# Two PSUM reads of a routing step move from VectorE to ScalarE, and TensorE turns the numbers earlier in its step

## The chip, the cores and the metric

The kernel runs on one core of one Trainium2 chip. The metric is device microseconds of one execution, median of three runs. A core has TensorE (PE in the profile; PEld is its weight load), VectorE (DVE), ScalarE (ACT), GpSimd (POOL) and SyncE (SP, which here only issues DMAs). Each engine works through its own instructions in the order in which they were issued to it; a semaphore wait holds one engine and everything that stands behind the wait on that engine.

## The reference

The input is 16 sequences of 512 tokens with 128 features. Each sequence passes causal attention with 16 heads of 8 features, a layer norm, a product-key mixture of experts (8 heads, 32 + 32 keys, the best 8 of 64 pairs, 1,024 experts), and a second layer norm.

```python
q, k = _rope(_rms_norm(q, q_norm_w), _rms_norm(k, k_norm_w), cos, sin)
attn = softmax(where(causal, -inf, einsum('bhqd,bhkd->bhqk', q, k) * scale))
x = _layernorm(x + einsum('bhqk,bhkd->bhqd', attn, v)... @ w_proj.T)
...
xn = _rmsnorm(x, norm_w)
q = (xn @ w_q.T).reshape(b, t, H, 2, DK)
s1, i1 = top_k(einsum('bthd,hkd->bthk', q[..., 0, :], keys[:, :, 0, :]), K)
s2, i2 = top_k(einsum('bthd,hkd->bthk', q[..., 1, :], keys[:, :, 1, :]), K)
all_idx = (i1[..., :, None] * NKEYS + i2[..., None, :]).reshape(b, t, H, K * K)
all_sc = (s1[..., :, None] + s2[..., None, :]).reshape(b, t, H, K * K)
fs, pk = top_k(all_sc, K)
fi = take_along_axis(all_idx, pk, axis=-1)
hidden = gelu(einsum('btd,bthkd->bthk', xn, expert_down[fi])) * relu(fs)
x = _layernorm(x + einsum('bthk,bthkd->btd', hidden, expert_up[fi]))
```

## The kernel before, in words

One pass of the loop (`iteration`) works on up to five sequences at once, each at another stage: `b` is in attention, `nxt` is having its q and k made, `late` (b-1) is in the norm and the choice of experts, `older` (b-2) in the experts' weights, `oldest` (b-3) in the last product and norm. With 16 sequences there are 19 passes; 2 to 14 hold nearly all stages, pass 15 has no `nxt`, and pass 16 has no attention of its own. The order on each engine is written out by hand, in one function `iteration` for each engine. TensorE and ScalarE count 40 steps in a pass, one per unit of attention scores.

TensorE, at each step: the scores of the step into one of two PSUM banks `S`; at steps 27, 31, 35 and 39 (`QK_STEPS`) the transposes of `nxt`'s stacked q and k into the same two banks (`transpose_stack`); at most steps one of 32 parts of `weights(older)`, which multiplies one-hot rows of experts by their weights into a bank `G`; and `late`'s work on its selection. `turn_numbers(late, t)` transposes the chosen experts' numbers of tile t, 20 matmuls, at steps 22, 28, 34 and 35 (`NUMBER_STEPS`). `transpose_selection`, two transposes at step 35, adds the chosen scores to the same bank, `F_SEL`. Part 28 of `weights`, at step 35, waits for `rows_done`: VectorE's last four one-hot blocks of `older`.

ScalarE: at each step the exponential of the scores (`prob<-S`); at QK_STEPS the copies of q and k from the banks (`qT`, `kT_even`, `kT_odd`). The scores of step 36 go to the bank that q was turned into and wait for the copy `qT`; those of step 37 go to k's bank and wait for `kT_odd`.

VectorE: sorts out the keys and pairs of `late` (`top_keys`, `top_pairs`), and makes the one-hots and weights of `older`. After `top_pairs(late, 3)` GpSimd's `gather` finishes the last tile of numbers, while VectorE makes one-hots 28 to 31 and applies a chunk of weights. Then `decode(late)` reads `F_SEL` and splits each expert number into a low and a high part (`elo`, `ehi`) and each weight into three bf16 parts (`wpart`), and the first one-hots of that sequence follow. `eint`, the whole numbers, lies in the memory of `hot_hi`; so the trace calls it `hot_hi`.

Of the kernel before, what the change touches and what calls it, by code (L numbers as in the profile page):

```python
# [39 lines left out]
def attention_then_peer_layer(nc, x, w_qkv, w_proj, q_norm_w, k_norm_w, w_q, keys, expert_down, expert_up,  # L40
# [3 lines left out]
    ALU, ACT, AX = mybir.AluOpType, mybir.ActivationFunctionType, mybir.AxisListType  # L44

    P = 128
# [21 lines left out]
    with ctx:  # L68
# [137 lines left out]
        def signal(name, per_batch, seed=0):  # L206
            return Signal(sem(name), per_batch, seed)
# [37 lines left out]
        sel_ready = signal("sel_ready", 1)  # L245
# [10 lines left out]
        numbers_turned = signal("numbers_turned", NT)  # L256
        hid_done = signal("hid_done", NHI, 2)
        dec = signal("dec", 4, 4)
        hi_done = signal("hi_done", 4)
        hot_done = signal("hot_done", 4)  # L260
        rows_done = signal("rows_done", 1)
# [289 lines left out]
        def _(act):  # L551
# [11 lines left out]
            def hidden(b, c):  # L563
                act.wait_ge(hid_ready.sem, hid_ready.value(b, c + 1))
                act.activation(hid[:, c, :], bank_hid(c)[:, :], ACT.Gelu).then_inc(hid_done.sem, 1)  # L565

            def taken_x(b):
                act.wait_ge(xT_ready.sem, xT_ready.value(b, 1))
                act.activation(xT[:, :], bank_s("xT", 0)[:, :], ACT.Copy).then_inc(xT_done.sem, 1)
# [90 lines left out]
            def iteration(b, late, older, oldest, nxt):  # L660


                if late is not None:
                    attended(late, NG - 1)
                if b is not None:
                    taken_v(b)
                if nxt is not None:
                    taken_x(nxt)
                for n in range(NG * UNITS):
                    if b is not None:  # L670
                        exps(b, n // UNITS, [n % UNITS])
                    if n == 3:
                        if nxt is not None:
                            taken_qk(nxt, 0)
                            taken_qk(nxt, 1)
                        if late is not None:
                            taken_outputs(late)
                    if n == 4 and older is not None:
                        for c in range(NHI):
                            hidden(older, c)  # L680
                    if n == 7 and late is not None:
                        normed(late)
                    if late is not None and n in (8, 9):
                        similarities(late, n - 8)
                    if nxt is not None and n in (13, 17):
                        first_parts(nxt, (n - 13) // 4)
                    if n == 12 and late is not None:
                        norm1_rows(late)
                    if n == 13 and oldest is not None:
                        norm2_rows(oldest)  # L690
                    if nxt is not None and n in (20, 21):
                        second_parts(nxt, n - 20)
                    if late is not None and n in (14, 17):
                        similarities(late, 2 + (n - 14) // 3)
                    if nxt is not None and n in QK_STEPS:
                        transposed(nxt, QK_STEPS.index(n), b is not None)
                    if b is not None and n in (9, 19, 29):
                        attended(b, n // UNITS)
# [14 lines left out]
        def _(pe):  # L713
# [211 lines left out]
            def iteration(b, late, older, oldest, nxt, shifted):  # L925
# [9 lines left out]
                for step in range(NG * UNITS):  # L935
# [11 lines left out]
                    if step == 4:  # L947
# [5 lines left out]
                            expert_outputs(oldest, range(2, NT))  # L953
                        if older is not None:
                            hidden_products(older)
                    if nxt is not None and step in QK_STEPS:
                        transpose_stack(nxt, QK_STEPS.index(step), b)
                    if older is not None and step in WEIGHT_STEPS:
# [4 lines left out]
                        transpose_o(b, g - 1)  # L963
                    if late is not None and step in SIMS_STEPS:
                        project_similarities(late, SIMS_STEPS.index(step))
                    if late is not None and step in NUMBER_STEPS:
                        turn_numbers(late, NUMBER_STEPS.index(step))
                    if late is not None and step == SELECTION_STEP:
                        transpose_selection(late)
                    if b is not None and u == UNITS - 1 and g < NG - 1:  # L970
                        attend(b, g)
                if nxt is not None and shifted:
# [52 lines left out]
        def _(dve):  # L1025
# [192 lines left out]
            def decode(b):  # L1218
# [2 lines left out]
                twice = lambda a: a.unsqueeze(2).to_broadcast([P, n, 2])  # L1221
                pairs = lambda a: a.rearrange("p a t c -> p (a t) c")
                flat = lambda a: a.rearrange("p a t c -> p (a t c)")
                e, w = F_SEL[:, 0:n], F_SEL[:, n:2 * n]
                w0, w1, w2 = (pairs(wpart[:, i]) for i in range(3))
                rest = wrest[:, :, :].rearrange("p a t -> p (a t)")
                dve.wait_ge(sel_ready.sem, sel_ready.value(b, 1))
                dve.tensor_copy(pairs(eint[:, :, :, :]), twice(e))
                dve.tensor_scalar(w0, twice(w), 0.0, None, ALU.max).then_inc(dec.sem, 1)
                dve.wait_ge(dec.sem, dec.value(b, 1))  # L1230
                dve.tensor_scalar(flat(elo[:, :, :, :]), flat(eint[:, :, :, :]), P - 1, None, ALU.bitwise_and)
                dve.tensor_scalar(flat(ehi[:, :, :, :]), flat(eint[:, :, :, :]), NEXP - P, None, ALU.bitwise_and)
                dve.scalar_tensor_tensor(rest, w, 0.0, w0[:, :, 0], ALU.max, ALU.subtract)\
                    .then_inc(dec.sem, 1)
                dve.wait_ge(dec.sem, dec.value(b, 2))
# [231 lines left out]
```

## Time and profile before

| | |
|---|---|
| three runs | 1601.63, 1603.32, 1605.12 us; median 1603.32 us |
| the profiled execution | 1606.01 us |
| its span, first to last instruction | 1604.2 us |
| busy: PE, DVE, ACT, POOL | 85%, 85%, 57%, 41% of the span |
| mean granted clock of TensorE | 0.89 of full speed |
| one pass in the steady part | 90.3 to 90.6 us |

The busy shares are over the whole span, start-up and the last passes included. What a change in one place is worth has to be read from the instructions there.

### The profile page before, as it was taken

What the parts mean: (1) busy time and instruction counts of PE and PEld (TensorE: products, weight loads), DVE (VectorE), ACT (ScalarE), POOL (GpSimd) and SP (SyncE); (2) the same over time, 40 slices, a digit from 0 to 9 for tenths busy, and PEclk for the clock granted to TensorE, in tenths of its full rate; (3) what the DMA queues carried; (4) which work ended last, traced back from release to release, by engine and by line L of the source; (5) the groups of instructions that cost most, each with busy time, mean ns of one, the idle gap of its engine ahead of it and who ended that gap; (6) DMA issues with size and microseconds to landing.
All of it is one profiled execution on the core that took longest, in us unless ns stands there. A gap on an engine that the chain in (4) does not pass through costs nothing.

```text
span 1604.2 us, 55167 instructions
## 1 busy us (share of the span) xinstructions
PE 1356.4 (85%) x21008; PEld 976.6 (61%) x21008; DVE 1362.6 (85%) x6576; ACT 918.0 (57%) x1494; POOL 663.9 (41%) x1024
## 2 busy tenths in 40 slices
PE   5676879989898989989898989989898988978567
PEld 4342547666666747666666747666675756665456
DVE  5307689989999999989999998989999998798984
ACT  3665757666666667666666657666666656532110
POOL 3306263462708263461708264461708264150510
PEclk7777989989998989989898989989898989988666
DMA  3000000000000000000000000000000000000000
GB/s 86 7 8 8 8 9 9 16 2 9 16 9 16 9 15 9 16 2 9 16 9 16 9 15 10 15 3 9 16 9 16 2 15 3 14 3 2 9 1 17
DMA packets 29989, 18.81 MB, mean 12 GB/s; under 512 B 1824, under 2 KB 29216, under 8 KB 29728
## 3 DMA queue, kind: packets, MB, share of 16 engines
q1 hardware_dynamic: 29728, 15.23, 3.3%
q8 instruction: 176, 2.88, 0.8%
q14 instruction: 85, 0.70, 0.1%
HBM read 11.04 MB, written 4.19 MB: 9 GB/s over the span
## 4 chain that ended last, share of the span: by engine, by line
PE 39%; DVE 37%; issue 8%; ACT 8%; POOL 6%; DVEq 0%; ACTq 0%; POOLq 0%
DVE onehot L1246 10%; PE G L921 8%; PE F L866 7%; PE OV L810 6%; DVE topi L1192 6%; PE G L910 5%; DVE psel L1208 4%; DVE topv L1186 3%; DVE whot L1271 3%; ACT prob L636 3%; PE S L796 3%; DVE fsel L1203 2%; DVE hid L1284 2%; PE S L735 2%; PE F L876 2%
## 5 line engine op out<-in xcount | busy, mean ns | idle before, releaser
L636 ACT ACTIVATE prob<-S 128x512 f32<-128x512 f32 x640 | 371.0, 596 | 148.5 <-PE S L798 142.3
L910 PE MATMUL G<-whot,onehot 128*128 128x16 bf16 x12288 | 384.4, 171 | 31.1 <-DVE hid L1284 19.0
L910 PEld LDWEIGHTS G<-whot,onehot 128*128 128x128 bf16 x12288 | 365.5, 97 | 66.5 <-issue 18.0
L1246 DVE TENSOR_TENSOR onehot<-lo_no,elo 128x1024 bf16<-128x1024 uint16 x512 | 384.6, 803 | 0.0
L810 PE MATMUL OV<-prob,vp 128*9 128x512 f32 (+3 forms) x2048 | 183.4, 508 | 65.3 <-ACT prob L636 59.7
L500 POOL TENSOR_TENSOR gat<-gat,cande 128x1280 f16<-128x1280 f16 x64 | 178.5, 2789 | 77.8 <-DVE gat L1214 77.8
L798 PE MATMUL S<-causal,ident_b 128*128 128x128 bf16 x1024 | 203.0, 231 | 0.0
L796 PE MATMUL S<-qT,kT_even 128*128 128x512 bf16 (+3 forms) x512 | 147.3, 316 | 54.9 <-ACT prob L636 46.5
L509 POOL COPY y<-y_new 128x512 f32<-128x512 f32 x16 | 9.8, 610 | 434.3 <-DVE r L1170 376.5
L565 ACT ACTIVATE hid<-F 128x512 f32<-128x512 f32 x128 | 76.5, 597 | 189.0 <-PE F L866 189.0
L810 PEld LDWEIGHTS OV<-prob,vp 128*9 128x9 f32 x2048 | 55.3, 100 | 195.1 <-issue 106.5
L1192 DVE FIND_INDEX8 topi<-topv,sims 128x8 uint16<-128x32 f32 x1024 | 166.2, 185 | 2.2 <-issue 2.1
L796 PE MATMUL S<-qT,kT_odd 128*128 128x256 bf16 (+3 forms) x512 | 152.2, 324 | 14.7 <-ACT kT_odd L620 8.6
L447 POOL TENSOR_TENSOR gat<-qk_r,cosw 128x256 f32<-128x256 f32 x64 | 73.7, 1152 | 207.3 <-DVE yi L1156 177.5
L921 PE MATMUL G<-up,hid 128*128 128x128 f32 x1024 | 125.9, 284 | 10.3 <-DVE hid L1284 10.3
L1271 DVE TENSOR_TENSOR whot<-hot_hi,wpart 128x1024 bf16<-128x1024 bf16 x192 | 130.1, 732 | 2.2
L921 PEld LDWEIGHTS G<-up,hid 128*128 128x128 f32 x1024 | 122.6, 200 | 10.4 <-DVE hid L1284 10.4
L643 ACT ACTIVATE oT<-OV 128x512 f32<-128x512 f32 x64 | 38.2, 597 | 154.8 <-PE OV L810 153.4
L1284 DVE TENSOR_TENSOR hid<-G,hid 128x512 f32<-128x512 f32 x128 | 87.5, 684 | 35.2 <-PE G L910 35.2
L796 PEld LDWEIGHTS S<-qT,kT_even 128*128 128x128 bf16 x512 | 50.5, 99 | 109.5 <-ACT prob L636 63.3
L866 PE MATMUL F<-xn,downT 128*128 128x512 f32 x256 | 117.2, 611 | 0.0
L480 POOL TENSOR_SCALAR i<-topi 128x64 f16<-128x64 uint16 x128 | 64.7, 525 | 125.8 <-DVE topi L1192 125.6
(138 smaller groups left out, 2499.3 us busy)
## 6 DMA issues: line engine op xcount, KB each, us to landing
xa<-in_L_attn_x SPq DMA_DIRECT2D x16, 256.0 KB, 2.9
xr<-in_L_attn_x SPq DMA_DIRECT2D x16, 256.0 KB, 2.9
out<-r SPq DMA_DIRECT2D x16, 256.0 KB, 2.3
onehot<-in_L_ffn_expert_down SPq DMA_DIRECT2D x1, 512.0 KB, 5.2
up<-in_L_ffn_expert_up SPq DMA_DIRECT2D x1, 512.0 KB, 7.6
onehot<-in_L_ffn_keys SPq DMA_DIRECT2D x1, 256.0 KB, 4.3
onehot<-in_L_attn_w_qkv SPq DMA_DIRECT2D x1, 192.0 KB, 3.1
onehot<-in_L_attn_w_proj SPq DMA_DIRECT2D x1, 64.0 KB, 5.3
```

Of the source, the lines that this page charges most:

```text
L500: pool.tensor_tensor(g, g, cande[:, t % 2].rearrange("p h c -> p c h").unsqueeze(3) .to_broadcast([P, NCAND, H, TOPK]), ALU.mult)\
L636: act.activation(dst, src, ACT.Exp, scale=SCALE).then_inc(exp_done.sem, 1)
L796: nc.tensor.matmul(bank[:, col:col + T - kc * P], pe_k, qT[:, j, kc * P:T], start=True, stop=False, skip_group_check=True)
L798: last = nc.tensor.matmul(bank[:, col:col + P], ident_b[:, :], causal[:, :], start=False, stop=True, skip_group_check=True)
L810: last = nc.tensor.matmul(OV[32 * i:32 * i + HD + 1, kc * P:T], vp[:, kc, 4 * g + i, :], prob[:, i, KC_AT[kc]:KC_AT[kc] + T - kc * P], sta ...
L866: nc.tensor.matmul(bank_hid(c)[:, :], downT[:, c * P:(c + 1) * P], xn[:, :], start=True, stop=True)\
L910: last = nc.tensor.matmul(bank[:, 16 * i:16 * i + 16], onehot[:, row, :], whot[:, t, w_part, :], start=(w_part == 0), stop=(w_part == 2))
L921: last = nc.tensor.matmul(OUT[:, t * P:(t + 1) * P], hid[:, c, t * P:(t + 1) * P], up[:, c, :], start=(c == 0), stop=(c == NHI - 1))
L1192: last = dve.max_index(topi[:, t, s, h, :], topv[:, t, s, h, :], sims[:, t % 2, s, h, :])
L1246: return dve.tensor_tensor(onehot[:, row:row + 8, :].rearrange("p t (c i) -> p t c i", i=2), lo, e, ALU.is_equal)
L1271: last = dve.tensor_tensor(whot[:, t0:t0 + 64, part, :].rearrange("p t (c i) -> p t c i", i=2), hot, wpart[:, part, pair, t0:t0 + 64].unsq ...
L1284: dve.tensor_tensor(h, g, h, ALU.mult).then_inc(g_free.sem, 1)
```

## The change

VectorE's two reads of the bank at the head of `decode` go to ScalarE, as `taken_selection`: a copy of the numbers with cast to `eint` and the first weight part through Relu, in ScalarE's order at step 35, behind that step's exponential and ahead of the copies of q and k. VectorE's `decode` now waits for them. On TensorE `turn_numbers` and `transpose_selection` are called ahead of `transpose_stack` and `weights` of the same step. The number of instructions on TensorE, GpSimd and SyncE stays.

```diff
+            def taken_selection(b):
+                n = 2 * P
+                act.wait_ge(sel_ready.sem, sel_ready.value(b, 1))
+
+                if not (isinstance(b, int) and b == 0):
+                    act.wait_ge(hot_done.sem, hot_done.value(b - 1, 4))
+                act.activation(eint[:, :, :, :].rearrange("p a t c -> p (a t) c"),
+                               F_SEL[:, 0:n].unsqueeze(2).to_broadcast([P, n, 2]), ACT.Copy).then_inc(eint_done.sem, 1)
+                act.activation(wpart[:, 0].rearrange("p a t c -> p (a t) c"),
+                               F_SEL[:, n:2 * n].unsqueeze(2).to_broadcast([P, n, 2]), ACT.Relu).then_inc(dec.sem, 1)
...
+                    if late is not None and n == SELECTION_STEP:
+                        taken_selection(late)
                     if nxt is not None and n in QK_STEPS:
                         transposed(nxt, QK_STEPS.index(n), b is not None)
...
+                    if late is not None and step in NUMBER_STEPS:
+                        turn_numbers(late, NUMBER_STEPS.index(step))
+                    if late is not None and step == SELECTION_STEP:
+                        transpose_selection(late)
                     if nxt is not None and step in QK_STEPS:
                         transpose_stack(nxt, QK_STEPS.index(step), b)
                     if older is not None and step in WEIGHT_STEPS:
...
-                    if late is not None and step in NUMBER_STEPS:
-                        turn_numbers(late, NUMBER_STEPS.index(step))
-                    if late is not None and step == SELECTION_STEP:
-                        transpose_selection(late)
...
-                dve.wait_ge(sel_ready.sem, sel_ready.value(b, 1))
-                dve.tensor_copy(pairs(eint[:, :, :, :]), twice(e))
-                dve.tensor_scalar(w0, twice(w), 0.0, None, ALU.max).then_inc(dec.sem, 1)
-                dve.wait_ge(dec.sem, dec.value(b, 1))
+                if not (isinstance(b, int) and b == 0):
+                    dve.wait_ge(rows_done.sem, rows_done.value(b - 1, 1))
+                dve.wait_ge(eint_done.sem, eint_done.value(b, 1))
                 dve.tensor_scalar(flat(elo[:, :, :, :]), flat(eint[:, :, :, :]), P - 1, None, ALU.bitwise_and)
                 dve.tensor_scalar(flat(ehi[:, :, :, :]), flat(eint[:, :, :, :]), NEXP - P, None, ALU.bitwise_and)
+                dve.wait_ge(dec.sem, dec.value(b, 1))
```

On TensorE, step 35 of a full pass before: scores (`S<-qT,kT_even`), the transposes of q and of k (`S<-ident_b,stack`), part 28 of the weights (`G<-whot,onehot`), the numbers of tile 3 (`F<-ident_b,gat`) and the selection (`F<-ident,fsel`).

```order
L796 MATMUL S<-qT,kT_even 128x512 [waits exp_done]
L798 MATMUL S<-causal,ident_b 128x128
L746 MATMUL S<-ident_b,stack 128x128 [waits exp_done,stack_done]
L746 MATMUL S<-ident_b,stack 128x128 x7
L746 MATMUL S<-ident_b,stack 128x128 [waits exp_done]
L746 MATMUL S<-ident_b,stack 128x128 x7
L910 MATMUL G<-whot,onehot 128x16 [waits g_free,rows_done]
L910 MATMUL G<-whot,onehot 128x16 x23
L876 MATMUL F<-ident_b,gat 64x128 [waits gat_done]
L876 MATMUL F<-ident_b,gat 64x128 x19
L886 MATMUL F<-ident,fsel 128x128 [waits fsel_done]
L886 MATMUL F<-ident,fsel 128x128
```

The same step of the change:

```order
L810 MATMUL S<-qT,kT_even 128x512 [waits exp_done]
L812 MATMUL S<-causal,ident_b 128x128
L890 MATMUL F<-ident_b,gat 64x128 [waits gat_done]
L890 MATMUL F<-ident_b,gat 64x128 x19
L900 MATMUL F<-ident,fsel 128x128 [waits fsel_done]
L900 MATMUL F<-ident,fsel 128x128
L760 MATMUL S<-ident_b,stack 128x128 [waits exp_done,stack_done]
L760 MATMUL S<-ident_b,stack 128x128 x7
L760 MATMUL S<-ident_b,stack 128x128 [waits exp_done]
L760 MATMUL S<-ident_b,stack 128x128 x7
L924 MATMUL G<-whot,onehot 128x16 [waits g_free,rows_done]
L924 MATMUL G<-whot,onehot 128x16 x23
```

The 22 matmuls of numbers and selection moved from behind the wait for `rows_done` to a place ahead of the transposes of q and k.

On ScalarE, the end of step 35 and the start of step 36 in the change: the exponential of step 35, the two new reads (`hot_hi<-F` is `eint`, `wpart<-F` the first weight part), then the copies of q and k, which before stood right behind the exponential.

```order
L648 ACTIVATE prob<-S 128x512 [waits s_ready]
L574 ACTIVATE hot_hi<-F 128x512 [waits hot_done,sel_ready]
L576 ACTIVATE wpart<-F 128x512
L622 REGISTER_ALU
L623 ACTIVATE qT<-S 128x1024 [waits qk_turned]
L628 REGISTER_ALU
L631 ACTIVATE kT_even<-S 64x1024 [waits qk_turned]
L632 ACTIVATE kT_odd<-S 64x1024
L639 REGISTER_ALU [waits pv_done]
L648 ACTIVATE prob<-S 128x512 [waits s_ready]
```

The copies of q and k now stand behind a wait for `sel_ready`, TensorE's selection of the same step. ScalarE has eight table loads in its program before and eight after.

## Rows read from the trace of the kernel before

**Rows 1.** Timeline, VectorE: start, us, engine, line, operation, [idle before <-releaser]
```profile
846.58 1.59 DVE L1186 MAX8 topv<-sims 128x8 f32<-128x32 f32 x16 [0.35 <-ACT sims L560]
```
**Rows 2.** Timeline, TensorE, steps 35 to 39 of one steady pass
```profile
805.57 0.39 PE L796 MATMUL S<-qT,kT_even 128*128 128x512 bf16 x1
...
807.90 0.77 PE L910 MATMUL G<-whot,onehot 128*128 128x16 bf16 x24 [0.58 <-DVE onehot L1246]
808.60 1.30 PE L876 MATMUL F<-ident_b,gat 128*64 128x128 bf16 x20
809.83 0.44 PE L886 MATMUL F<-ident,fsel 128*128 128x128 f32 x2
...
811.05 0.27 PE L796 MATMUL S<-qT,kT_even 128*128 128x256 bf16 x1
...
812.86 0.32 PE L796 MATMUL S<-qT,kT_odd 128*128 128x384 bf16 x1
```
**Rows 3.** Timeline, ScalarE, the same steps
```profile
806.05 0.60 ACT L636 ACTIVATE prob<-S 128x512 f32<-128x512 f32 x1 [1.60 <-PE S L798]
806.55 1.02 ACT L611 ACTIVATE qT<-S 128x1024 bf16<-128x1024 bf16 x1
...
808.48 1.02 ACT L620 ACTIVATE kT_odd<-S 64x1024 bf16<-64x1024 bf16 x1
```
**Rows 4.** Timeline, VectorE, the same steps: one-hots 28 to 31, then decode
```profile
803.21 4.64 DVE L1246 TENSOR_TENSOR onehot<-lo_no,elo 128x1024 bf16<-128x1024 uint16 x4
...
810.31 0.69 DVE L1228 CAST hot_hi<-F 128x512 uint16<-128x512 f32 x1 [1.86 <-PE F L886]
...
811.63 0.30 DVE L1231 TENSOR_SCALAR elo<-hot_hi 128x512 uint16<-128x512 uint16 x1
...
813.57 4.90 DVE L1246 TENSOR_TENSOR onehot<-lo_no,elo 128x1024 bf16<-128x1024 uint16 x8
```
**Rows 5.** Timeline, GpSimd: the last gather of the pass
```profile
802.88 2.61 POOL L500 TENSOR_TENSOR gat<-gat,cande 128x1280 f16<-128x1280 f16 x1 [0.94 <-DVE gat L1214]
```
**Rows 6.** Timeline, TensorE, steps 35 and 39 of the next pass
```profile
896.48 0.39 PE L796 MATMUL S<-qT,kT_even 128*128 128x512 bf16 x1
...
898.50 0.76 PE L910 MATMUL G<-whot,onehot 128*128 128x16 bf16 x24 [0.26 <-DVE onehot L1246]
...
903.45 0.32 PE L796 MATMUL S<-qT,kT_odd 128*128 128x384 bf16 x1
```
**Rows 7.** Timeline, TensorE's weight loads: turn_outputs at step 3
```profile
823.41 0.42 PEld L827 LDWEIGHTS A<-ident,o 128*128 128x128 f32 x4 [0.37 <-DVE o L1122]
```
**Rows 8.** Timelines, passes 15 and 16: decode, and TensorE's next wait for VectorE
```profile
1437.51 2.60 POOL L500 TENSOR_TENSOR gat<-gat,cande 128x1280 f16<-128x1280 f16 x1 [0.93 <-DVE gat L1214]
...
1446.21 0.69 DVE L1228 CAST hot_hi<-F 128x512 uint16<-128x512 f32 x1 [3.15 <-PE F L886]
...
1443.21 2.34 PE L876 MATMUL F<-ident_b,gat 128*64 128x128 bf16 x20
...
1459.34 1.09 PE L827 MATMUL A<-ident,o 128*128 128x128 f32 x4 [5.33 <-DVE o L1122]
...
1534.17 0.69 DVE L1228 CAST hot_hi<-F 128x512 uint16<-128x512 f32 x1 [3.19 <-PE F L886]
...
1545.51 2.71 PE L921 MATMUL G<-up,hid 128*128 128x128 f32 x11 [9.47 <-DVE hid L1284]
```
**Rows 9.** Timeline, ScalarE, pass 1: the exponentials of steps 36 to 39
```profile
180.70 2.48 ACT L636 ACTIVATE prob<-S 128x512 f32<-128x512 f32 x4
```
**Rows 10.** Windows, TensorE: us, busy (instructions), granted clock, DMA share, GB/s
```profile
767.50:769.80 2.30, 0.01 (x1) 1.00 0.00 0
771.00:781.00 10.00, 6.87 (x86) 0.50 0.03 11
```
**Rows 11.** Timeline, TensorE: the same 32 matmuls of attention at two times
```profile
777.15 4.25 PE L810 MATMUL OV<-prob,vp 128*9 128x512 f32 x32 [3.13 <-ACT prob L636]
...
814.87 2.34 PE L810 MATMUL OV<-prob,vp 128*9 128x512 f32 x32 [0.21 <-issue]
```

More of the change, by code:

```diff
@@ L258, in attention_then_peer_layer @@
         dec = signal("dec", 4, 4)
+        eint_done = signal("eint_done", 1)
         hi_done = signal("hi_done", 4)
@@ L1223, in decode @@
                 flat = lambda a: a.rearrange("p a t c -> p (a t c)")
-                e, w = F_SEL[:, 0:n], F_SEL[:, n:2 * n]
+                w = F_SEL[:, n:2 * n]
                 w0, w1, w2 = (pairs(wpart[:, i]) for i in range(3))
                 rest = wrest[:, :, :].rearrange("p a t -> p (a t)")
-                dve.wait_ge(sel_ready.sem, sel_ready.value(b, 1))
-                dve.tensor_copy(pairs(eint[:, :, :, :]), twice(e))
-                dve.tensor_scalar(w0, twice(w), 0.0, None, ALU.max).then_inc(dec.sem, 1)
-                dve.wait_ge(dec.sem, dec.value(b, 1))
+                if not (isinstance(b, int) and b == 0):
+                    dve.wait_ge(rows_done.sem, rows_done.value(b - 1, 1))
+                dve.wait_ge(eint_done.sem, eint_done.value(b, 1))
                 dve.tensor_scalar(flat(elo[:, :, :, :]), flat(eint[:, :, :, :]), P - 1, None, ALU.bitwise_and)
                 dve.tensor_scalar(flat(ehi[:, :, :, :]), flat(eint[:, :, :, :]), NEXP - P, None, ALU.bitwise_and)
+                dve.wait_ge(dec.sem, dec.value(b, 1))
                 dve.scalar_tensor_tensor(rest, w, 0.0, w0[:, :, 0], ALU.max, ALU.subtract)\
```

## The prediction

> **What bounds the kernel now.** The page's shares, 85% for TensorE and for VectorE, name no bound by themselves. I first read what VectorE waits for at the start of the key sorting, since one pass is the distance between two such starts. It waits 0.35 us for ScalarE's copy of the similarities [rows 1]. So a pass ends with TensorE and ScalarE, and VectorE comes 0.35 us too early. From there the chain of waits runs through VectorE's sorting, and through ScalarE to the attention matmuls; then it splits. TensorE goes on to step 35 by itself; VectorE goes through the pair sorting to one-hots 28 to 31, which end at 803.21 + 4.64 = 807.85. Both meet at weights part 28, where TensorE waits 0.58 us for the one-hots [rows 2, 4]. In the next pass this wait is 0.26 us [rows 6]; the two kinds of pass alternate, 13 in all (2 to 14). Then come numbers (1.23 us to the next start), selection and the scores of steps 36 to 39, and TensorE and ScalarE run on to the next similarities. The 1.86 us that VectorE stands before decode [rows 4] is therefore not the price of a pass: VectorE has 0.35 us to spare at the end of the same stretch even with that wait in it.
>
> **What the change does to VectorE.** It loses two instructions, 811.63 - 810.31 = 1.32 us a pass, and most of its wait. Numbers can start right after the scores of step 35, at about 805.57 + 0.34 = 805.91: the last gather ends at 802.88 + 2.61 = 805.49 [rows 2, 5]. Selection then ends 1.23 + 0.44 = 1.67 us later [rows 2], at 807.58, ScalarE's first read at about 808.24. VectorE is free at 810.31 - 1.86 = 808.45 and starts `elo` without waiting, against 811.63 before: 3.2 us earlier. In a steady pass I cost this gain at nothing but what follows: VectorE's next work for TensorE is `o` of the last group, and TensorE's weight load there waits 0.37 us for it [rows 7], of which the matmul loses about 0.15 us, since the matmuls before it end almost as late. Beyond that VectorE waits longer at the similarities.
>
> **What it does to TensorE and ScalarE.** TensorE's matmuls are the same; their order isn't. ScalarE gets two instructions more in a place where it was on its way to the copies of q and k, and these two wait for the selection. Nothing in the trace shows a ScalarE copy with this operand; the nearest rows are its exponential of a 128x512 bank, 0.60 us and 0.50 us to the next start, and the two VectorE instructions that it replaces, 0.69 us each [rows 3, 4]. I take 0.50 each, as source, size and engine agree; 0.69 is the upper bound, and 0.3, as for a 128x512 instruction of SBUF on VectorE (`elo` [rows 4]), the lower.
>
> Relu brings no table load: the program has eight before and after. Then, counted in one pass:
> - Selection ends at 807.58; the first read starts at about 807.64, the second at 808.13, `qT` at 808.62. Before, `qT` started at 806.55 [rows 3].
> - `qT`, `kT_even` and `kT_odd` take 808.48 + 1.02 - 806.55 = 2.95 us from start to end as before, so `kT_odd` ends at about 811.57 instead of 809.50.
> - The scores of step 37 need the bank that `kT_odd` reads. They start at 811.61 instead of 811.05 [rows 2]. TensorE, which then ends part 28 at about 809.0 and part 29 at 810.6, stands about 1 us there, and 0.7 us before step 36 for `qT`, which ends at 809.64; before, it did not wait at either.
> - Steps 37 to 39 keep their pace, 812.86 - 811.05 = 1.81 us, so step 39 comes at 813.42 instead of 812.86: **0.56 us later**, although part 28 no longer waits and numbers and selection no longer stand behind it.
>
> The next pass, of the other kind, has 903.45 - 896.48 = 6.97 us from the scores of step 35 to those of step 39 [rows 6], against 7.29 here, and the new chain is the same 7.85 us in both: 0.88 us later. Minus 0.15 us at `turn_outputs`, a steady pass gets 0.41 or 0.73 us longer, 0.57 us on the mean. Over 13 passes: **+7.4 us**. With the bounds of the copies (two times 0.3 or 0.69 instead of 0.50) it is 0.17 to 0.95 us a pass, +2 to +12 us.
>
> The other moves: numbers of tiles 0, 1 and 2 now stand ahead of one weights part of 24 matmuls. They were all gathered earlier, and the part that comes 1.23 us later is needed by VectorE only after its four one-hots of 4.64 us [rows 4]; nothing.
>
> **First and last passes.** In pass 1 no weights are computed, and the exponentials of steps 36 to 39 run without a gap [rows 9], so ScalarE sets the end of the pass. It is held by the two reads and by the wait for selection, as above 808.62 - 806.55 = 2.1 us; bounds 1.0 (the reads alone) and 2.1. I take **+1.9 us**, a bit under the upper one because the last gather is long done there.
>
> In passes 15 and 16 no copies of q and k follow, and VectorE ends the chain: it stands 3.15 and 3.19 us before decode, and TensorE later waits 5.33 and 9.47 us for VectorE [rows 8]. In pass 15 the gather ends at 1440.11; numbers take 2.34 us there, selection and read about 1.2, so `elo` starts near 1443.7. VectorE was free at 1446.21 - 3.15 = 1443.06 and reached `elo` 1.32 us after 1446.21, at 1447.53. That is 3.8 us earlier; the last of decode waits some 0.1 us for the second read: **-3.7 us**. In pass 16, with the gather as long before the wait, I take **-3.1 us**. Bounds: 1.3 (only the two instructions) and 4.5 us (the whole wait too) in each.
>
> Sum: 7.4 + 1.9 - 3.7 - 3.1 = +2.5 us. On the profiled execution's 1606.0 us this is 1608.5; that execution lies 2.7 us above the median of the runs, so on the median it is **1605.8 us**. Within 0.2% (3.2 us) of before is about what a measurement here can't tell from no change.
>
> **A rule against it.** The two VectorE instructions take 1.32 us and ScalarE's exponential of the same bank size 0.60 us [rows 3, 4], so by the rows ScalarE isn't the dearer engine. The Trainium skill (ScalarE: Activation LUTs, Rules for kernel authors) sends relu and max to VectorE, which it calls up to about three times as fast per element in bf16. If each read took three times VectorE's 0.69 us, 2.07 us, a pass would be 2 x (2.07 - 0.50) = 3.1 us longer still and the kernel 41 us slower, 1647 us. The source here is fp32 in PSUM, where the trace agrees with no such factor; 1 in 100.
>
> **Rivals.**
> - *The clock falls in the new gap.* TensorE had the higher clock (1.00, 2.4 GHz) before it stood still from 767.5 to 769.8, and 0.50, 1.2 GHz, from 771 to 781 after [rows 10]; the same 32 attention matmuls take 4.25 us there and 2.34 us at the higher clock [rows 11]. The change puts two stands, 0.7 and 1.0 us, within 2.6 us before the last group's attention. For it: together they near the 2.3 us. Against: single stands of 0.6 us, as at part 28, left the clock alone. Where it falls, attention costs 1.9 us more. In 3 or 4 of 13 passes that is 6 to 8 us: 1612 us; in all, 1631.
> - *Faster by the path.* If ScalarE doesn't hold steps 36 and 37, TensorE runs from step 35 to 39 without a stand: it saves the wait for `rows_done` (0.58 or 0.26 us) and small gaps for k, about 0.7 us a pass, 9 us, with the 6.8 of the last passes and without the 1.9 of the first 1588 us. For it: ScalarE stood 1.60 us before the exponential of step 35 [rows 3]. Against: its order is fixed, and the copies can't start before selection. It decides once the reads and the wait for selection together stay under 2.07 - 0.56 = 1.5 us.
> - *Steady passes unchanged.* A pass is held elsewhere too, in the slower attention and in the sorting, and absorbs 0.5 us; then only the ends remain: 1603.3 + 1.9 - 6.8 = 1598.4 us.
> - *A later gather.* Numbers of tile 3 have 805.91 - 805.49 = 0.4 us to spare [rows 2, 5]. If GpSimd is later by more, TensorE stands in front of the transposes and ScalarE in front of its copies; each further 0.5 us costs 6.5 us: 1612 us.
>
> **How the numbers follow.** The sum as worked out 45% (1602 to 1610, so half of it within 0.2%, nearly all the rest slower); the clock 24% (1607 to 1620); unchanged steady passes 16%, mostly faster by a little over 0.2%; the faster path 8%; a later gather 6%; the rule 1%. Faster: 12 + 7 + 1 = 20%. Same: 24 + 4 + 4 = 32%. Slower: 48%. The range leaves out the faster path's lower end, and the clock falling in most passes: 1596 to 1616 us.
>
> **What would show it.** VectorE's two instructions are gone, and decode waits under 0.5 us instead of 1.86. ScalarE's two reads take 0.6 us each and end before `qT`, which starts about 2 us later after the step-35 exponential. TensorE waits for `qT` at step 36 and for `kT_odd` at step 37, and not for the one-hots at part 28. VectorE waits over 1 us for the similarities instead of 0.35. A steady pass is 90.8 to 91.3 us, against 90.3 to 90.6. I am wrong if the scores of steps 36 and 37 wait for nothing, if passes come out shorter than 90.4 us, or if the clock's low stretches multiply.

## The result, and the profile after

| | before | after |
|---|---|---|
| median, same chip | 1603.38 us (1601.63 to 1605.12) | 1618.91 us (1618.64 to 1620.39) |
| ratio | 1 | 1.0093, 95% interval 1.0078 to 1.0107 |
| span of the profiled execution | 1604.2 us | 1618.6 us |
| steady pass, mean of 12 | 90.41 us | 92.14 us |

The change makes the kernel 0.9% slower. The forecast was slower, but by 0.2%: 1605.8 us, with a range that ends at 1616. So the sign is right, and a part of the price is missing. Of the experiments' runs one counts as slow, 1665.57 us of kernel 3, and is left out below.

**Where the 14.4 us are.** Between the starts of the key sorting, which I again take as the ends of passes, the two profiled executions differ by 12 x 1.73 = +20.8 us in the steady passes, +3.3 in the last full one (pass 14; 95.84 against 92.55), +0.1 in pass 1, -5.2 in pass 15 (86.11 against 91.34), -3.2 from there to the end, and -1.3 in start-up. So the main thing to be explained is the steady pass. (In pass 14 the steady price comes again, and 1.26 us more behind the last group's attention, where in the change alone the clock is low once more, from 91.1 us after the sorting's start.) What answers to [rows 1] (VectorE):

```profile
765.65 1.59 DVE L1200 MAX8 topv<-sims 128x8 f32<-128x32 f32 x16 [0.47 <-ACT sims L561]
```

The next such start is at 857.80; all steady passes are now alike, 92.11 to 92.20 us. Steps 35 to 39 of this pass on TensorE, as in [rows 2]:

```profile
815.57 0.38 PE L810 MATMUL S<-qT,kT_even 128*128 128x512 bf16 x1
...
815.93 1.30 PE L890 MATMUL F<-ident_b,gat 128*64 128x128 bf16 x20
817.17 0.44 PE L900 MATMUL F<-ident,fsel 128*128 128x128 f32 x2
817.44 1.06 PE L760 MATMUL S<-ident_b,stack 128*128 128x128 bf16 x16
818.34 0.75 PE L924 MATMUL G<-whot,onehot 128*128 128x16 bf16 x24
819.70 0.34 PE L810 MATMUL S<-qT,kT_even 128*128 128x384 bf16 x1 [0.61 <-ACT qT L623]
...
821.62 0.28 PE L810 MATMUL S<-qT,kT_even 128*128 128x256 bf16 x1 [0.83 <-ACT kT_odd L632]
...
823.73 0.48 PE L810 MATMUL S<-qT,kT_odd 128*128 128x384 bf16 x1
...
824.33 1.88 PE L760 MATMUL S<-ident_b,stack 128*128 128x128 bf16 x16
826.14 2.34 PE L824 MATMUL OV<-prob,vp 128*9 128x512 f32 x32
```

The wait for the one-hots at part 28 is gone, and TensorE stands 0.61 us before step 36 and 0.83 us before step 37 instead. Scores of step 37 come 821.62 - 815.57 = 6.05 us after those of step 35; the forecast was 6.04. ScalarE, as in [rows 3]:

```profile
817.64 0.60 ACT L574 ACTIVATE hot_hi<-F 128x512 uint16<-128x512 f32 x1 [1.00 <-PE F L900]
818.14 0.59 ACT L576 ACTIVATE wpart<-F 128x512 bf16<-128x512 f32 x1
818.61 1.03 ACT L623 ACTIVATE qT<-S 128x1024 bf16<-128x1024 bf16 x1
...
820.55 1.02 ACT L632 ACTIVATE kT_odd<-S 64x1024 bf16<-64x1024 bf16 x1
```

The two reads and the copies lie as forecast. What the forecast lacks starts behind step 37. From there on the same matmuls take longer: the scores of step 39 take 0.48 us instead of 0.32 [rows 2]. The windows of TensorE in this place say why (columns as in [rows 10]), here of the same steps and then of two more passes:

```profile
815.50:818.50 3.00, 3.00 (x56) 1.00 0.02 5
818.50:822.60 4.10, 2.66 (x81) 1.00 0.00 0
822.70:826.10 3.40, 3.40 (x47) 0.51 0.00 0
826.20:829.50 3.30, 3.30 (x42) 1.00 0.03 7
```

```profile
362.12:365.22 3.10, 3.10 (x45) 0.50 0.01 3
...
1283.51:1286.61 3.10, 3.10 (x45) 0.50 0.00 0
```

Right behind the two stands the granted clock falls from 1.00 to 0.50, that is from 2.4 to 1.2 GHz, and comes back before the attention matmuls, which take 2.34 us. It does so in each of the 13 passes 2 to 14; in the kernel before, the same place has 1.00 in every pass (one of 11 such windows):

```profile
812.14:815.24 3.10, 2.65 (x50) 1.00 0.00 0
```

VectorE reaches `elo` at 818.34, 2.77 us after the scores of step 35, where it took 6.06 us before [rows 2, 4]. The 3.3 us don't reach the end of the pass; they turn into other waits of VectorE (in the kernel before none at `rden`, 0.30 us at `r` and 0.31 at this `hid`):

```profile
818.34 0.29 DVE L1244 TENSOR_SCALAR elo<-hot_hi 128x512 uint16<-128x512 uint16 x1 [0.23 <-ACT hot_hi L574]
...
831.73 0.26 DVE L1134 RECIPROCAL rden<-A 128x16 f32<-128x16 f32 x1 [2.21 <-PE A L834]
...
843.91 0.69 DVE L1184 TENSOR_TENSOR r<-G,y 128x512 f32<-128x512 f32 x1 [0.85 <-PE G L935]
...
855.95 0.69 DVE L1298 TENSOR_TENSOR hid<-G,hid 128x512 f32<-128x512 f32 x1 [1.11 <-PE G L924]
```

### The profile page after: what moved, and what is told of

It reads as the page before. It is cut to its first block and busy times, and to the rows that moved or that the text cites. A ratio compares the mean times of both kernels' runs of the same rounds, so it can differ in the third digit from the quotient of the medians.

```text
span 1618.6 us, 55197 instructions
## 1 busy us (share of the span) xinstructions
PE 1356.9 (84%) x21008; PEld 974.9 (60%) x21008; DVE 1343.3 (83%) x6544; ACT 936.9 (58%) x1526; POOL 663.5 (41%) x1024
## 3 DMA queue, kind: packets, MB, share of 16 engines
q8 instruction: 176, 2.88, 0.7%
## 5 line engine op out<-in xcount | busy, mean ns | idle before, releaser
L448 POOL TENSOR_TENSOR gat<-qk_r,cosw 128x256 f32<-128x256 f32 x64 | 68.2, 1066 | 205.7 <-DVE yi L1170 175.6
```

## The experiments

**My theory after the result:** the loss of a steady pass has two parts, ScalarE's hold (the copies of q and k stand behind the selection and two reads; 0.6 us, as forecast) and the lower clock behind the stands that this makes. **Rivals:** TensorE's new order does it alone, whatever ScalarE does; the reads do it alone; VectorE's lost instructions matter.

| kernel | median (range), us | ratio, 95% interval | pass, mean of 12 |
|---|---|---|---|
| 1 order alone | 1609.25 (1608.35 to 1613.37) | 1.0037 [1.0023, 1.0051] | 91.33 |
| 2 stands filled, 20 matmuls | 1612.34 (1611.31 to 1615.69) | 1.0057 [1.0041, 1.0074] | 92.16 |
| 3 reads doubled | 1641.22 (1637.97 to 1658.37) | 1.0274 [1.0200, 1.0348] | 93.53 |
| 4 numbers between | 1598.1 (1593.25 to 1599.19) | 0.9953 [0.9935, 0.9971] | 90.42 |
| 5 between, reads behind | 1592.81 (1590.12 to 1595.21) | 0.9928 [0.9905, 0.9951] | 90.41 |
| 6 reads behind | 1626.41 (1624.88 to 1627.61) | 1.0141 [1.0120, 1.0161] | 92.47 |
| 7 filled, 2 matmuls | 1649.81 (1648.89 to 1651.85) | 1.0284 [1.0264, 1.0304] | 95.19 |
| 8 reads only | 1600.86 (1598.16 to 1604.63) | 0.9986 [0.9973, 0.9999] | 90.38 |
| 9 filled, fp32 in place | 1652.98 (1652.36 to 1654.41) | 1.0305 [1.0288, 1.0323] | 95.19 |
| 10 order filled, fp32 in place | 1649.77 (1649.37 to 1654.55) | 1.0292 [1.0274, 1.0311] | 94.87 |
| 11 filled, bf16 in place | 1611.55 (1610.18 to 1613.86) | 1.0060 [1.0043, 1.0077] | 91.09 |
| 12 order filled, bf16 in place | 1616.76 (1614.15 to 1623.05) | 1.0082 [1.0066, 1.0099] | 91.97 |

Ratios are to the kernel before on the same chip (its medians there 1602.48 to 1604.32 us). Pass times and clocks are those of one profiled execution of each kernel. In kernels 9 to 12 matmuls are replaced, so some tokens lack the second part of their weights there.

**1. TensorE's order alone.** The kernel before, with numbers and selection ahead of the transposes; VectorE reads.

```diff
+                    if late is not None and step in NUMBER_STEPS:
+                        turn_numbers(late, NUMBER_STEPS.index(step))
+                    if late is not None and step == SELECTION_STEP:
+                        transpose_selection(late)
                     if nxt is not None and step in QK_STEPS:
                         transpose_stack(nxt, QK_STEPS.index(step), b)
...
-                    if late is not None and step in NUMBER_STEPS:
-                        turn_numbers(late, NUMBER_STEPS.index(step))
-                    if late is not None and step == SELECTION_STEP:
-                        transpose_selection(late)
```

> TensorE's order of the change alone; VectorE reads the bank itself as before, ScalarE gets nothing. My theory (ScalarE's two reads ahead of its copies of q and k open a stand in front of steps 36 and 37, and the clock falls in it): the copies of q and k start about 1.5 us later than before, close to 808.1 in the pass that was read, the scores of step 37 at 811.1, where they were; no second low stretch of the clock in a pass; a pass of 90.3 to 90.7 us, 1597 to 1605 us in all. Rival (the order on TensorE costs, since the transposes of q and k come later): most of the loss stays, 1612 to 1619 us.

It is slower than before, so ScalarE's reads are not all of it; its time lies between the two ranges. Measured from the start of the numbers, the copy of q comes after 2.15 us here and after 2.68 us in the change, so the reads add 0.53 us to a delay that is mostly the order's. There is now one stand, 0.84 us before step 37. In ten of 12 passes the clock falls behind it, and these take 91.64 us on the mean; in the two without, 89.78 and 89.83 us. (The profiled execution is one of the two fastest of five runs; how many passes fall in the others is not known.) Windows of a pass of each kind, up to the stand and behind it:

```profile
628.00:632.40 4.40, 3.48 (x81) 1.00 0.01 4
632.40:635.80 3.40, 3.09 (x73) 1.00 0.00 0
718.80:724.00 5.20, 4.28 (x101) 1.00 0.01 3
724.50:727.80 3.30, 3.30 (x49) 0.50 0.00 0
```

**2, 7, 9 and 10. The stands filled, and a new one made.** TensorE gets matmuls whose result nobody reads, where it would stand. In the second kernel these are 8 and 12 bf16 matmuls behind parts 28 and 29, in the seventh one fp32 matmul behind each. The ninth has fp32 matmuls in place of small ones, and the tenth the same for order alone.

```diff
+            def fill(n, b):
+                pe.wait_ge(oT_done.sem, oT_done.value(b, NG - 1))
+                for _ in range(n):
+                    nc.tensor.matmul(OV[:, 0:P], ident_b[:, :], ident_b[:, :], start=True, stop=True,
+                                     skip_group_check=True)
...
                     if older is not None and step in WEIGHT_STEPS:
                         weights(older, WEIGHT_STEPS.index(step))
+                        if nxt is not None and step in (35, 36):
+                            fill((0, 8, 12)[step - 34], b)
```

> The change, and TensorE fills its stands in front of steps 36 and 37 with 8 and 12 small matmuls whose result nobody reads (0.5 and 0.7 us of work in stands of 0.61 and 0.83 us). The waits for ScalarE's copies stay as they are. My theory that the fall of the clock in the stand is more than half of the loss: the low stretch near step 38 disappears, a pass takes 90.9 to 91.2 us instead of 92.15, 1603 to 1609 us. Rival (the wait for the copies is the whole loss, the clock only follows): 1617 to 1621 us as the change, or more.

> The change with TensorE's two stands filled by one fp32 matmul each into a free bank (256 and 384 columns; 2 instructions more a pass, where the first filling had 20). Theory (the low clock behind the stands costs 0.6 to 0.8 us of a pass, and the longer stand of 0.8 to 1.3 us at the loop's head in the first filling came of the 20 instructions): the low stretch at step 38 is gone, attention of the last group starts about 6.8 us after the copy of q instead of 7.5, the stand at the loop's head is under 0.4 us, passes 91.2 to 91.6 us, 1603 to 1611 us. Rival (TensorE arrives at the loop's head before its instructions whatever fills the stands): the stand at the loop's head is 0.8 us or more, passes 91.8 to 92.4 us, 1611 to 1619 us. Rival (the clock costs nothing): passes 92.1 us with attention at 7.5 us.

> The change, with three of the 48 small matmuls of weights parts 28 and 29 replaced by fp32 matmuls of 256, 256 and 128 columns into columns of the same bank that are written later, so that TensorE works through most of its two stands with as many instructions as in the change (three tokens of a chunk lack the second part of their weights). Theory (the low clock behind the two stands costs 0.6 to 0.8 us of a pass, and the first two fillings lost it again because instructions were added to the loop): the stand at the loop's head is about 0.2 us, no low stretch at step 38, attention of the last group starts 6.8 to 6.9 us after the copy of q instead of 7.5, passes 91.2 to 91.6 us, 1605 to 1612 us. Rival (what the clock gives back is lost at the loop's head whatever fills the stands): the stand there is 0.8 us or more, and passes are 92 us or longer, 1616 us or more. Rival (the clock falls all the same): 1617 to 1621 us.

> The kernel before with TensorE's new order alone (VectorE reads), and two of the 24 small matmuls of weights part 29 replaced by fp32 matmuls of 256 and 128 columns in the same bank, so that the one stand of 0.84 us before step 37 is mostly filled with as many instructions. Theory (with the order alone the low clock behind that stand is the whole loss): every steady pass is 89.7 to 90.1 us, as the two passes without a low stretch were, and the time is 1585 to 1594 us, below the kernel before. Rival (the order costs through the later copies of q and k, not through the clock): passes 91 us or longer, 1602 to 1610 us.

In all four the scores of step 39 come 4.83 us after the copy of q, not 5.1 as in the change, and steps 38 and 39 are at 2.4 GHz. And in all four a pass of the loop is no shorter, since TensorE stands at the loop's head, before the last group's attention, for nothing that the profile shows: 0.8 to 1.35 us in the second, 2.3 to 3.8 us in the others, at each return to it. A row of the ninth kernel:

```profile
843.95 3.98 PE L824 MATMUL OV<-prob,vp 128*9 128x512 f32 x32 [3.29 <-issue]
```

The page has a trace of it. In its list of queues (packets, MB, share) the one that brings instructions moves this in the seventh, ninth and tenth kernel (187 packets and 3.06 MB in the second):

```profile
q8 instruction: 186, 3.05, 0.7%
```

and this in the change, in the fifth and in the last two:

```profile
q8 instruction: 176, 2.88, 0.7%
```

A packet is 2.88 MB / 176 = 16.4 KB, so these loops bring about one packet more in a pass. My "as many instructions" for the ninth and tenth was wrong: an fp32 matmul is more than one instruction of TensorE's code (the trace has two matmuls for each of these calls). The Trainium skill (Runtime: NRT & Kernel Launch, Instruction fetch mechanics) says that instructions come in blocks of 16 KiB, one after the other, and that a taken branch to a block that isn't there waits for it. The packet size and the place of the stand agree with that; what part of the 3.3 us is the block's way, no run here separates. In pass 14, where the loop is left, it is the other way round: these four have no stand ahead of the last group's attention, the kernel before has one of 3.18 us and the change one of 3.07.

What these four kernels were for, the price of the clock in a pass of the loop, they can't tell. Pass 2, ahead of the loop, has no such stand: it takes 90.08 us in the seventh and 90.11 in the ninth, against 92.20 in the change and 89.97 before. There almost the whole loss goes with the fall.

**11. The stands filled with code of the same length.** Nine of the small matmuls of parts 28 and 29 become wide bf16 ones.

```diff
                     for w_part in range(3):
+                        cols = {(28, 0, 1): 496, (28, 1, 1): 480, **{(29, i, 1): 256 for i in range(7)}}.get((part, i - 8 * quarter, w_part))
+                        if cols:
+                            nc.tensor.matmul(bank[:, 512 - cols:512], onehot[:, row, :],
+                                             whot[:, P - CHUNK:P, :, :].rearrange("p t w c -> p (t w c)")[:, 0:cols],
+                                             start=True, stop=True, skip_group_check=True)
+                            continue
```

> The change, with nine of the 48 small matmuls of weights parts 28 and 29 replaced by bf16 matmuls of 496, 480 and seven times 256 columns of the weights' own operands, into columns of the same bank that are written later, so that TensorE works through most of its two stands (nine tokens lack the second part of their weights). No fp32 matmul is added, so that TensorE's code has not only as many instructions but the same length as in the change; the earlier fillings made it 8 to 40 instructions of 64 bytes longer per pass. Theory (the stand of 3.3 us at the loop's head in the earlier fillings came of the longer code, and the low clock costs 0.6 to 0.9 us of a pass): the stand there is 0.2 us, no low stretch at step 38, attention 6.8 to 6.9 us after the copy of q, passes 91.0 to 91.5 us, 1603 to 1611 us. Rival (the stand at the loop's head comes whenever TensorE does not stand in the steps before it): it is 0.8 us or more again, passes 92 us or longer, 1612 us or more.

The theory holds in what it says of the stands, the clock and the pass; the time, 1611.55 us, lies 0.55 us beyond its range. Steps 36 to 39 of one pass on TensorE, and windows of two passes from step 38 on, which like those of the other passes have 1.00:

```profile
813.88 0.34 PE L810 MATMUL S<-qT,kT_even 128*128 128x384 bf16 x1 [0.25 <-ACT qT L623]
...
815.80 0.28 PE L810 MATMUL S<-qT,kT_even 128*128 128x256 bf16 x1 [0.24 <-ACT kT_odd L632]
...
817.63 0.32 PE L810 MATMUL S<-qT,kT_odd 128*128 128x384 bf16 x1
...
819.71 2.34 PE L824 MATMUL OV<-prob,vp 128*9 128x512 f32 x32 [0.28 <-issue]
```

```profile
361.66:364.76 3.10, 2.65 (x61) 1.00 0.01 3
...
1272.16:1275.26 3.10, 2.69 (x62) 1.00 0.00 0
```

The hold is still there: step 37 still waits for `kT_odd`. So a pass can be divided. Means of ten passes each (before from 394.64 to 1299.00 us, after from 397.14 to 1318.56, this one from 305.16 to 1215.66), worked out from the starts in the timelines:

| us | before | after | filled (11) |
|---|---|---|---|
| sorting to scores of step 35 | 49.59 | 49.92 | 49.47 |
| scores of step 35 to last group's attention | 9.14 | 10.56 | 9.92 |
| attention to next sorting | 31.71 | 31.67 | 31.66 |
| pass | 90.44 | 92.14 | 91.05 |

Without the fall of the clock the change costs 91.05 - 90.44 = **0.61 us** a pass; the forecast of the hold was 0.57. What goes with the fall is 92.14 - 91.05 = **1.09 us**: 0.64 in steps 38 and 39, the transposes and the way to attention, 0.45 in the first part of the pass. There TensorE is at 1.2 GHz for some time in all three kernels; where that begins varies from pass to pass with before and with this one, and hardly with the change. That this is a follow-up of the fall is argued, not shown. The ten passes of kernel 11 leave out its pass 13 (92.51 us), where the clock falls later, 87.8 us after the sorting's start; with it in the place of pass 3 the mean is 91.17 us and the two parts are 0.73 and 0.97 us. The whole run gains less than 13 such passes: the two profiled executions differ by 10.2 us, since start-up, pass 1 and the stretch from the last sorting to the end together take 4.1 us more than with the change, and by the ratios of the runs, 1.0093 and 1.0060, it is about 5 us. So the fall's price is shown in sign, and in size only for these executions.

**12. Order alone, filled in the same way** (seven matmuls of part 29).

> The kernel before with TensorE's new order alone (VectorE reads), and seven of the 24 small matmuls of weights part 29 replaced by bf16 matmuls of 256 columns in the same bank, with TensorE's code of the same length as before. Theory (with the order alone the low clock behind the one stand of 0.84 us is the whole loss): the stand at the loop's head is 0.2 us, steady passes are 89.7 to 90.2 us, 1585 to 1596 us. Rival (the later copies of q and k cost by themselves): passes 91 us or longer, 1602 to 1612 us. Rival (a stand at the loop's head whenever TensorE does not stand before it): that stand 0.8 us or more, passes 91.5 us or longer.

The theory fails here. The fall behind step 37 is gone, attention comes 6.85 us after the copy of q, and the passes in the loop take 92.0 to 92.3 us all the same: in 11 of 12 passes the clock now falls later, about 87.6 us after the sorting's start, and the way from attention to the next sorting takes 32.9 us instead of 31.66. The twelfth, ahead of the loop, takes 89.75 us. (The profiled execution, 1623.05 us, is the longest of the four; the others take 1614.15 to 1618.03 us.) Windows ahead of the later fall and in it:

```profile
850.00:852.90 2.90, 2.10 (x66) 1.00 0.02 6
853.10:856.40 3.30, 3.30 (x34) 0.50 0.00 0
```

So the price of TensorE's order by itself stays open: 89.8 us in two passes of kernel 1, but never steadily.

**3. Twice the reads.** ScalarE reads the numbers twice more into a spare tile.

```diff
+                for i in range(2):
+                    act.activation(spare_read[:, i, :].rearrange("p (n c) -> p n c", c=2),
+                                   F_SEL[:, 0:n].unsqueeze(2).to_broadcast([P, n, 2]), ACT.Copy)
```

> The change with two more ScalarE reads of the same bank and size ahead of the two, into a buffer that nobody reads. My theory that what stands ahead of the copies of q and k sets steps 36 and 37: about 1.0 us more on the scores of step 37 and on each of 13 steady passes, 1629 to 1635 us. Rival (ScalarE has room there, it idles 40% of the time, and the loss comes from the order on TensorE): 1617 to 1621 us.

The copy of q comes 0.96 us later, measured from the numbers, and TensorE's stand before step 36 grows from 0.61 to 1.59 us; the clock at step 39 is low again. A pass takes 93.53 - 92.14 = 1.39 us more. The time is longer than I expected for this: what ScalarE does ahead of its copies is paid in full, and more. The low stretch behind the stands is often longer here (6.8 instead of 3.4 us, in 8 of the 12 passes); that this is the rest of the 1.39 us is not shown, and the runs spread by 20 us.

```profile
831.71 0.34 PE L814 MATMUL S<-qT,kT_even 128*128 128x384 bf16 x1 [1.59 <-ACT qT L627]
```

**6. The reads behind the copies.** One call moves in ScalarE's order.

```diff
-                    if late is not None and n == SELECTION_STEP:
-                        taken_selection(late)
                     if nxt is not None and n in QK_STEPS:
                         transposed(nxt, QK_STEPS.index(n), b is not None)
+                    if late is not None and n == SELECTION_STEP:
+                        taken_selection(late)
```

> The change with ScalarE's two reads moved behind its copies of q and k; TensorE's order stays that of the change. Theory (each read ahead of the copies delays them by 0.5 us, and TensorE's order alone delays them by 1.2 to 1.6 us more): the copies start as with the order alone, about 0.5 us earlier than in the change, scores of step 37 about 5.2 us after the numbers' start instead of 5.7, and the low clock stays in most passes: 1607 to 1613 us. Rival (ScalarE's reads cost nothing, the order does all): as the change, 1616 to 1621 us. Rival (ScalarE's reads do all of it): as before, 1600 to 1605 us.

I was wrong here: it is slower than the change. ScalarE's rows show what I had left out:

```profile
823.39 0.60 ACT L574 ACTIVATE hot_hi<-F 128x512 uint16<-128x512 f32 x1
823.89 0.59 ACT L576 ACTIVATE wpart<-F 128x512 bf16<-128x512 f32 x1
824.36 1.09 ACT L648 ACTIVATE prob<-S 128x512 f32<-128x512 f32 x2
```

The scores of step 36 end long before, but their exponential starts behind the reads, 1.0 us later after the copy of q than in kernel 1, and the scores of step 38 go to the same bank. Step 39 comes 5.8 us after the copy of q, against 4.84 in the passes of kernel 1 with the high clock, and the clock falls in all 13 passes. With TensorE's order of the change neither of the two places that were tried on ScalarE is free.

**8. The reads only,** behind the copies, with TensorE's order as before.

> The kernel before with only the two reads moved to ScalarE, behind its copies of q and k; TensorE's order as before. Theory (VectorE's two instructions do not end a steady pass): steady passes 90.3 to 90.8 us as before, decode's wait stays near 2 us and VectorE waits longer at the similarities, the last passes gain about 1 us each: 1600 to 1604 us. Rival (VectorE's 1.32 us a pass count): passes 89.0 to 89.7 us, 1585 to 1594 us. Rival (the reads, which there wait for the selection behind weights part 28, hold the exponential of step 36): passes 91 to 92.5 us, 1610 to 1630 us.

VectorE is rid of 1.32 us a pass, and a pass takes 90.38 us instead of 90.41. The time goes into the wait for the reads:

```profile
805.67 0.29 DVE L1244 TENSOR_SCALAR elo<-hot_hi 128x512 uint16<-128x512 uint16 x1 [2.56 <-ACT hot_hi L574]
```

**4 and 5. Numbers and selection between the transposes and part 28,** so that ScalarE's copies are not held; in 4 VectorE reads, in 5 ScalarE, behind its copies.

```diff
                     if nxt is not None and step in QK_STEPS:
                         transpose_stack(nxt, QK_STEPS.index(step), b)
+                    if late is not None and step in NUMBER_STEPS:
+                        turn_numbers(late, NUMBER_STEPS.index(step))
+                    if late is not None and step == SELECTION_STEP:
+                        transpose_selection(late)
                     if older is not None and step in WEIGHT_STEPS:
...
-                    if late is not None and step in NUMBER_STEPS:
-                        turn_numbers(late, NUMBER_STEPS.index(step))
-                    if late is not None and step == SELECTION_STEP:
-                        transpose_selection(late)
```

> Numbers and selection between the transposes of q and k and the weights part; VectorE reads the bank itself as before. My theory: the copies of q and k stay where they were (qT 0.5 us after the exponential of step 35), numbers and selection fill the wait for the one-hots at part 28, the scores of step 36 start 0.5 to 0.6 us earlier than before; a pass of 89.8 to 90.1 us, and VectorE reads 1.3 us earlier in the last passes: 1590 to 1598 us. Rival (a pass is held elsewhere): 1601 to 1605 us.

> Numbers and selection stand between the transposes of q and k and weights part 28, and ScalarE does the two reads, but behind its copies of q and k. Theory (ScalarE's place ahead of the copies and TensorE's order ahead of the transposes cost the time, VectorE's two instructions do not end a steady pass): steady passes stay at 90.1 to 90.9 us as with VectorE reading itself, the copies start as in the kernel before, VectorE's decode starts its elo about 1.3 us earlier, and only the last two passes gain, 1 to 2 us: 1594 to 1599 us. Rival (VectorE's decode does end a pass once TensorE's order is better): steady passes fall by 0.6 to 1.3 us, 1582 to 1590 us. Rival (ScalarE's reads hold the exponential of step 36 behind the copies): passes 91 us or longer, 1603 to 1610 us.

Both are faster than before, and 5 is the fastest kernel of this study: 0.9928 [0.9905, 0.9951]. For 4 I had expected shorter passes, 89.8 to 90.1 us; they are not (90.42). The steady pass of 5 is that of before (90.41 us); it gains 6.3 us in pass 15 (85.02 us), 3.8 us behind it and 2.0 us in start-up, which differs by up to 4.0 us between these kernels and is no gain of the edit. On TensorE nothing waits for ScalarE's copies, and on ScalarE the reads lie where it would wait for the scores of steps 36 and 37:

```profile
807.55 0.32 PE L810 MATMUL S<-qT,kT_even 128*128 128x384 bf16 x1
...
808.49 0.27 PE L810 MATMUL S<-qT,kT_even 128*128 128x256 bf16 x1
```

```profile
806.65 1.02 ACT L632 ACTIVATE kT_odd<-S 64x1024 bf16<-64x1024 bf16 x1
807.69 0.60 ACT L574 ACTIVATE hot_hi<-F 128x512 uint16<-128x512 f32 x1
808.19 0.59 ACT L576 ACTIVATE wpart<-F 128x512 bf16<-128x512 f32 x1
808.66 1.82 ACT L648 ACTIVATE prob<-S 128x512 f32<-128x512 f32 x3
```

From the copy of q to the last group's attention it takes 7.6 us, against 8.0 to 8.3 before; every second pass gives 1.2 us back later, where the clock falls near its end and attention to sorting takes 32.9 us. These kernels also show that a loop in which steps 36 and 37 wait for nothing needn't stand at its head: 0.20 to 0.31 us there.

## Why the prediction was wrong

**The step that failed** is the rival of the clock. I had written of the two stands "together they near the 2.3 us" of a stand that does bring the clock down, and "single stands of 0.6 us, as at part 28, left the clock alone", gave the fall 24 in 100, and had it in 3 or 4 of 13 passes. The stands came as forecast (0.61 and 0.83 us; 0.7 and 1.0 forecast), and the clock fell in 13 of 13. The sum held the fall at nothing, and "3 or 4" had no ground in any row. The price was wrong in the other direction. I took 1.9 us for a slow attention; here the low stretch ends before attention, and kernel 11 puts it at 1.09 us a pass. 13 x 1.09 = 14 us would have made the forecast about 1620. That this comes so near 1618.91 is partly luck: the ends cost 4.7 us less than forecast (start-up counted), and pass 14 cost 1.6 us more than a steady pass.

Point by point:
- *VectorE's gain is worth nothing in a steady pass:* right (kernel 8, 90.38 us). Where it goes was wrong: I expected over 1 us of wait at the similarities; it is 0.47 us, and the rest is at `rden`, `r` and `hid`.
- *Of the gain of 0.15 us at `turn_outputs`* 0.04 arrived between attention and the next sorting.
- *The reads:* 0.60 and 0.59 us busy, 0.50 and 0.47 to the next start; right.
- *The chain of the copies:* right to 0.01 us at step 37. *A steady pass +0.57 us:* 0.61 to 0.73 with the clock left high (kernel 11), and 0.1 in pass 2.
- *Pass 1 +1.9 us:* measured +0.1. The hold is there (the copy of q starts 47.88 us after the sorting's start instead of 46.55, attention 0.76 us later still), and 2.0 us come back behind it, where the clock is low for less time: in the kernel before first, then in the change.

```profile
207.60:214.30 6.70, 5.20 (x57) 0.50 0.00 0
```

```profile
208.40:211.60 3.20, 3.20 (x32) 0.50 0.00 0
```

- *Pass 15 -3.7 us:* measured -5.2. The numbers of the last tile take 1.30 us there instead of the 2.34 that I took over [rows 8], and the gather starts 0.65 us earlier in the pass. *Pass 16 -3.1:* measured -3.2.
- *The rule against it* gave 2.07 us for a read and 1647 us in all. The Trainium skill's factor of three (ScalarE: Activation LUTs, Rules for kernel authors) is for bf16; the trace has 0.60 us on ScalarE for what took VectorE 0.69 [rows 4].
- *Faster by the path:* its condition, that ScalarE doesn't hold steps 36 and 37, is what kernels 4 and 5 bring about. The steady pass doesn't get shorter even then.
- *A later gather:* no. Numbers follow the scores of step 35 without a wait.

## What to carry to other kernels

When a change makes TensorE stand, price not only the stand but the clock behind it, and give a ground for the share of passes in which it is to fall (here it fell in 13 of 13, in kernel 1 in ten of 12); then look at the granted clock right behind the stand, in each pass. Before a piece of work goes ahead of another engine's copies, ask what waits for these copies: here 1.2 us of reads cost a steady pass nothing one place further back, once TensorE's selection had moved to where it held nobody. In a steady pass the time that was taken from VectorE only moved its waits.

## What the runs showed of the hardware that I had not expected

- A stand of 0.84 us alone (kernel 1) was followed by 1.2 GHz in ten passes of 12, with the same work in the two others; and a fall that was filled away at one place came back at another (kernel 12, 87.6 us into the pass). So these rows give no rule by which one stand brings the clock down.
- In this loop a few instructions more went with 0.8 to 3.8 us a pass at its head, with about one packet of 16.4 KB more in the instruction queue for each pass. An experiment that fills a gap here has to keep the length of the code, and that queue's row on the page told the kernels with the stand from those without.
